# Gated cross-attention and top-2 expert layer on one Trainium2 core: a changed order of first maxima and weights, and a second expert product in rounded part and rest

## What is computed

```python
# attention with gate
Q, K, V = ln(x) @ Wq + bq, ctx @ Wk + bk, ctx @ Wv + bv      # 16 heads of 16
attn = softmax(Q @ K.T / sqrt(16))
x = x + tanh(g_xattn) * ((attn @ V) @ Wo + bo)
# experts with gate
xf = ln(x)
scores = softmax(xf @ w_router.T); weights, idx = top_k(scores, 2)
h = silu(xf @ w1[e]) * (xf @ w3[e]); y = h @ w2[e]           # e over the two experts
x = x + tanh(g_ffn) * sum(weights * y)
```

## Time and profile before

| | us |
|---|---|
| median of 3 runs | 851.28 (850.83 to 853.52) |
| the profiled execution | 846.11 |
| its span | 844.4 |
| attention, from the first exponents to the last values | about 43 to 560 |
| expert tiles | about 560 to 836 |
| PE busy | 805.9 (95%) |
| DVE, ACT, POOL busy | 489.9, 441.4, 525.0 |

### The profile page before, as it was taken

The page is one execution under the profiler, slowest core; times in us unless marked ns, Lnnn a source line. Parts: engine busy times, 40 slices in busy tenths (PEclk is TensorE's granted clock), DMA queues, the critical chain, the costliest instruction groups (busy, mean ns, idle before and its releaser), DMA issues.

```text
span 844.4 us, 22220 instructions
## 1 busy us (share of the span) xinstructions
PE 805.9 (95%) x7529; PEld 698.5 (83%) x7529; DVE 489.9 (58%) x1170; ACT 441.4 (52%) x1120; POOL 525.0 (62%) x599
## 2 busy tenths in 40 slices
PE   7889999999999999999999999889999999999994
PEld 6789998999999999999999998767777777777773
DVE  5566777877777777777777777634622222222221
ACT  3356676676676677677666766555222222222221
POOL 6555565476667657666665765346677765656652
PEclk8989999999999999999999999999999999999998
DMA  5867777786676666676557566764443444434432
GB/s 158 191 150 174 197 185 192 180 205 156 171 176 158 169 165 158 153 178 154 136 147 175 139 156 138 213 146 79 57 60 62 75 64 64 64 62 65 64 57 30
DMA packets 99845, 112.33 MB, mean 133 GB/s; under 512 B 29276, under 2 KB 81124, under 8 KB 99736
## 3 DMA queue, kind: packets, MB, share of 16 engines
q1 hardware_dynamic: 79720, 92.48, 44.2%
q0 software_dynamic: 18512, 17.60, 13.5%
q10 hardware_dynamic: 1504, 0.85, 0.4%
HBM read 35.48 MB, written 17.53 MB: 63 GB/s over the span
## 4 chain that ended last, share of the span: by engine, by line
PE 78%; DVE 14%; issue 3%; DMA 2%; SPq 1%; ACT 1%; POOL 1%; ACTq 0%; POOLq 0%; DVEq 0%
PE ps L1474 18%; PE ps L1535 10%; PE ps L1198 9%; PE ps L1215 9%; PE ps L1229 7%; DVE negmax L922 7%; PE ps L1183 7%; PE ps L1330 3%; PE ps L1389 3%; PE ps L1222 3%; PE ps L1493 2%; PE ps L1418 2%; PE ps L1322 1%; DVE xa L907 1%; PE ps L1304 1%
## 5 line engine op out<-in xcount | busy, mean ns | idle before, releaser
L922 DVE TENSOR_REDUCE negmax<-ps 112x2 f32<-112x750 f32 x256 | 239.8, 938 | 110.4 <-PE ps L1215 109.2
L623 ACT ACTIVATE probs<-ps 125x448 f32<-125x448 f32 x384 | 209.6, 547 | 67.6 <-PE ps L1183 63.1
L402 POOL DMA_DIRECT2D stack<-negmax_t x128 | 68.0, 535 | 164.3 <-ACT negmax_t L678 153.1
L1183 PE MATMUL ps<-stack 97*125 97x224 f32 x768 | 166.5, 299 | 2.6 <-DMA stack<-negmax_t 1.8
L1215 PE MATMUL ps<-stack 96*112 96x376 f32 x512 | 140.5, 356 | 12.6 <-DVE negmax L922 11.8
L526 POOL DMA_INDIRECT out_dram<-y,idx x63 | 100.8, 1600 | 70.0 <-issue 30.9
L1183 PEld LDWEIGHTS ps<-stack 97*125 97x125 f32 x768 | 125.3, 189 | 9.3 <-DMA stack<-negmax_t 1.9
L722 ACT ACTIVATE silu<-ps 128x352 f32<-128x352 f32 x63 | 29.3, 465 | 184.4 <-PE ps L1474 184.4
L1134 DVE TENSOR_TENSOR h<-silu,ps 128x352 f32<-128x352 f32 x63 | 32.8, 521 | 147.3 <-PE ps L1474 147.2
L1535 PE MATMUL ps<-w_sb,h_t 128*128 x378 | 92.3, 380 | 0.7 <-ACT h_t L728 0.7
L1215 PEld LDWEIGHTS ps<-stack 96*112 96x112 f32 x512 | 71.5, 177 | 22.9 <-DVE negmax L922 19.8
(11 more groups left out here) (239 smaller groups left out, 1514.3 us busy)
## 6 DMA issues: line engine op xcount, KB each, us to landing
stack<-split SPq DMA_DIRECT2D x252, 150.0 KB, 2.9
stack<-split SPq DMA_DIRECT2D x127, 94.0 KB, 2.6
ctx_raw<-in_ctx_dram SPq DMA_DIRECT2D x29, 375.0 KB, 3.8
stack<-split SPq DMA_DIRECT2D x127, 56.0 KB, 2.8
out_dram<-xa SPq DMA_DIRECT2D x32, 112.0 KB, 2.5
xn_scratch<-xn SPq DMA_DIRECT2D x32, 112.0 KB, 2.2
xa<-in_x_dram SPq DMA_DIRECT2D x7, 448.0 KB, 4.2
w_sb<-in_L_ffn_w_dram SPq DMA_DIRECT2D x16, 176.0 KB, 2.8
```

The costliest lines, as they stand in the source:

```text
L402: gp.dma_start(dst[:, :, SKP + SQ * h:SKP + SQ * h + SQ], negmax_t[4 * h:4 * h + 4, half, :].bitcast(f32)).then_inc(s_nmrow[half][c % NSLO ...
L623: act.activation(probs[:, n % NP, :], ps[0:KW, EXPB + k % 2, 0:4 * SQ], ACT.Exp).then_inc(s_exp, 1)
L922: dve.tensor_reduce(negmax[:, half, :, p4], ps[0:SQ, m1:m2 + 1, 0:SK], axis=AX.X, op=ALU.max, negate=True).then_inc(s_max, 1)
L1183: last = pe.matmul(ps[0:KW, EXPB + k % 2, QW * m:QW * m + QW], stack[:, place_of(b), p, KW * ch:KW * ch + KW], stack[:, place_of(b), p, SK ...
```

## The change

Three parts. (1) In sub-step 0 of each step `maxes(c, 0)` goes ahead of `exps(b, 0)`. (2) The weights: w3's second half waits until the first half of the last batch's maxima rows has landed (three experts of it, the rest also for the end of batch 30's exponents); w2's first chunk is no longer loaded there, but with the other two chunks in step 31; PE waits for w1 alone ahead of its first w1 product, and for w3 ahead of the first w3 product. (3) From tile 13 on (50 of the 63) the second product is made from float32r parts: w2 is split once, in tiles 4 to 11, an expert at a time, by ACT (`w2_h`, a rounded copy, two instructions) and DVE (`w2_l`, the rest, two instructions); for each tile ACT's copy of the turned h is rounded (`ht_h`), DVE writes the rest (`ht_l`), and PE makes nine matmuls: ht_h with w2_h, ht_h with w2_l, ht_l with w2_h. To make room, `ctx_l`, `ctx_h`, `ctx_raw` and `probs` join the tensors whose memory is reused.

```diff
+        ctx_l, ctx_h = (late.enter_context(nc.sbuf_tensor(n, [P, NSLOT, DC, SKP], f32r)) for n in ("ctx_l", "ctx_h"))
+        ctx_raw = late.enter_context(nc.sbuf_tensor("ctx_raw", [P, DC, SK], f32))
+        probs = late.enter_context(nc.sbuf_tensor("probs", [KW, NP, 4 * SQ], f32))
         late.close()
...
+        ht_h, ht_l = (sb(n, [P, FC, P], f32r) for n in ("ht_h", "ht_l"))
+        w2_h, w2_l = (sb(n, [P, FC, NE, EMB], f32r) for n in ("w2_h", "w2_l"))
...
+        SPLIT, PARTS = 4, 13
...
+        def w2_parts(e):
+            n = F - P * (FC - 1)
+            return [tuple(w[:, 0:FC - 1, e, :] for w in (w2_sb, w2_h, w2_l)), tuple(w[0:n, FC - 1, e, :] for w in (w2_sb, w2_h, w2_l))]
...
@@ SP @@
                     sp.wait_ge(s_stack[(B - 1) % NSLOT], stacked(B - 1))
+                    sp.wait_ge(s_w13, 16 * DC * NE)
                     for e in range(NE):
                         sp.dma_start(w3_lo[:, e, :], w3[e, 0:P, :]).then_inc(s_w13, 16)
-                    first_weights()
+                    sp.wait_ge(s_exp_ps, 12 * (B - 2) + 6)
+                    sp.wait_ge(s_nmrow[0][(B - 1) % NSLOT], 32 * ((B - 1) // NSLOT + 1))
+                    for e in range(NE):
+                        if e == 3:
+                            sp.wait_ge(s_exp_ps, 12 * (B - 1))
+                        sp.dma_start(w3_hi[:, e, :], w3[e, P:2 * P, :]).then_inc(s_w13, 16)
...
                     sp.wait_ge(s_nmrow[1][(B - 1) % NSLOT], 32 * ((B - 1) // NSLOT + 1))
-                    for c in range(1, FC):
+                    for c in range(FC):
@@ ACT @@
-                    act.activation(h_t[:, :, :], ps[:, HTB, 0:FC * P], ACT.Copy).then_inc(s_h_t, 1)
+                    if t - 1 < PARTS:
+                        act.activation(h_t[:, :, :], ps[:, HTB, 0:FC * P], ACT.Copy).then_inc(s_h_t, 1)
+                    else:
+                        act.activation(ht_h[:, :, :], ps[:, HTB, 0:FC * P].rearrange("p (c q) -> p c q", c=FC), ACT.Copy).then_inc(s_h_t, 1)
+                if 0 <= t - SPLIT < NE:
...
+                    for raw, high, low in w2_parts(t - SPLIT):
+                        act.activation(high, raw, ACT.Copy).then_inc(s_w2h, 1)
@@ DVE @@
+                if t - 1 >= PARTS:
+                    dve.wait_ge(s_h_t, t)
+                    dve.tensor_tensor(ht_l[:, :, :], ps[:, HTB, 0:FC * P].rearrange("p (c q) -> p c q", c=FC), ht_h[:, :, :].bitcast(f32),
+                                      ALU.subtract).then_inc(s_htl, 1)
                 if t < TILES:
                     dve.wait_ge(s_silu, t + 1)
...
+                if 0 <= t - SPLIT - 1 < NE:
+                    for n, (raw, high, low) in enumerate(w2_parts(t - SPLIT - 1)):
+                        dve.wait_ge(s_w2h, 2 * (t - SPLIT - 1) + n + 1)
+                        dve.tensor_tensor(low, raw, high.bitcast(f32), ALU.subtract).then_inc(s_w2l, 1)
@@ PE @@
+                    if k == 0 and c is not None:
+                        maxes(c, 0)
                     if b is not None:
                         exps(b, k)
-                    if k in MAX_IN and k != 5 and c is not None:
+                    if k in MAX_IN and k not in (0, 5) and c is not None:
                         maxes(c, MAX_IN.index(k))
...
-                        pe.wait_ge(s_w13, 16 * 4 * NE)
+                        pe.wait_ge(s_w13, 16 * DC * NE)
...
+                    wait(pe, s_htl, o - PARTS)
                     for c in range(FC):
                         last = pe.transpose(ps[:, HTB, P * c:P * c + P], h[:, P * c:P * c + P], ident[:, :])
...
+                    if m == 0:
+                        pe.wait_ge(s_w13, 16 * 2 * DC * NE)
                     inner(m, (w3_lo, w3_hi), BB, e_m, s_b)
...
-                        pe.wait_ge(s_w2, 16 * (NE + FC - 1))
+                        pe.wait_ge(s_w2, 16 * FC)
                         pe.wait_ge(s_pv_t, B)
                     pe.wait_ge(s_h_t, o + 1)
                     wait(pe, s_y, o)
-                    for c in range(FC):
-                        n = min(P, F - P * c)
-                        last = pe.matmul(ps[:, YB, 0:EMB], h_t[0:n, c, :], w2_sb[0:n, c, bass.ds(e_o, 1), :].rearrange("p e d -> p (e d)"),
-                                         start=(c == 0), stop=(c == FC - 1))
+                    if o == PARTS:
+                        pe.wait_ge(s_w2l, 2 * NE)
+                    wait(pe, s_htl, o - PARTS + 1)
+                    terms = ((h_t, w2_sb),) if o < PARTS else ((ht_h, w2_h), (ht_h, w2_l), (ht_l, w2_h))
+                    for j, (ht, w) in enumerate(terms):
+                        for c in range(FC):
+                            n = min(P, F - P * c)
+                            last = pe.matmul(ps[:, YB, 0:EMB], ht[0:n, c, :], w[0:n, c, bass.ds(e_o, 1), :].rearrange("p e d -> p (e d)"),
+                                             start=(j + c == 0), stop=(j == len(terms) - 1 and c == FC - 1))
                     last.then_inc(s_y_ps, 1)
```

More of the change, by code:

```diff
@@ L69, in flamingo @@
         half2, lnv2, lnr2, lnt2 = (sb(n, [SQ, 1]) for n in ("half2", "lnv2", "lnr2", "lnt2"))
-        ctx_l, ctx_h = sb("ctx_l", [P, NSLOT, DC, SKP], f32r), sb("ctx_h", [P, NSLOT, DC, SKP], f32r)
         xn, xn_t = sb("xn", [SQ, EMB]), sb("xn_t", [P, DC, SQ])
@@ L78, in flamingo @@
         NP = 14
-        probs = sb("probs", [KW, NP, 4 * SQ])
         pv_t = sb("pv_t", [P, 4, SQ])
@@ L113, in flamingo @@
         iota_i = staged[0][:, 2560:2560 + P].bitcast(i32)
-        ctx_raw = sb("ctx_raw", [P, DC, SK])
         pad_tab = w1_sb[0:ROWS // 256, 0].rearrange("p e f -> p (e f)")[:, 0:4 * P].bitcast(i32).rearrange("p (a b c) -> p a b c", a=2, c=2)
@@ L134, in flamingo @@
         s_x = [sem(f"s_xload{n}") for n in range(4)]
+        s_w2h, s_w2l, s_htl = sem("s_w2h"), sem("s_w2l"), sem("s_htl")
         s_chi, s_clo, s_whi, s_wlo = (sem(n) for n in ("s_chi", "s_clo", "s_whi", "s_wlo"))
@@ L266, in load_idx @@
                              ).then_inc(s_idx_in[t % NIS], 16)
-            def first_weights():
-                for n in range(2 * NE):
-                    sp.wait_ge(s_exp_ps, 12 * (B - 2) + 3 * n // 4 + 1)
-                    e = n % NE
-                    if n < NE:
-                        sp.dma_start(w3_hi[:, e, :], w3[e, P:2 * P, :]).then_inc(s_w13, 16)
-                    else:
-                        sp.dma_start(w2_sb[:, 0, e, :], w2[e, 0:P, :]).then_inc(s_w2, 16)
             for i in range(FIRST, LAST + 1):
@@ L727, in _ @@
                     wait(act, s_y_ps, t - 1)
-                    act.activation(h_t[:, :, :], ps[:, HTB, 0:FC * P], ACT.Copy).then_inc(s_h_t, 1)
+                    if t - 1 < PARTS:
[3 more added lines that the diff above has]
+                if 0 <= t - SPLIT < NE:
+                    if t == SPLIT:
+                        act.wait_ge(s_pv, 4 * B)
+                        act.wait_ge(s_w2, 16 * FC)
+                    for raw, high, low in w2_parts(t - SPLIT):
+                        act.activation(high, raw, ACT.Copy).then_inc(s_w2h, 1)
                 if t == 3:
```

## The result

The changed kernel takes 872.05 us (median of 4 runs, 871.38 to 872.57) against 851.06 (4 runs) for the kernel before, run beside it: ratio 1.0246 (95% interval 1.0218 to 1.0274), 21.0 us slower. Its profiled execution took 872.02 (span 870.3).

A forecast was written before the change was run, and what follows sets the result against it. PE was taken to bound the steady tiles (busy 197.00 of 197.00 us). Terms -0.3 + 1.9 + 0.6 + 12 + 0.5 = +14.7 us, added to the median 851.28, gave 866.0, range 849 to 877.

The forecast's parts named there:

- the main term: Late tiles' w2 product from float32r parts: sequencer sends behind the wait for DVE's rest lengthen each tile, +12 us.
- The w2 product from parts, +12: Tiles 13 to 62: nine sends, read and address follow the wait; +0.25 in 48 turns, outer bounds -1 to +35.
- The first rival: Late tiles: sequencer is not the bound, PE's shorter work sets the period; total 844 to 849, chance 0.20.
- The weights, +1.9: Transition from attention to tiles: w2 lands near 573.1 against use at 571.22; +1.9 us, bounds -1.5 to +6.
- late next: First w2 product: w2's later landing cancels the about 1 us kept from the earlier maxima's rows.
- The price of the third chunk, 3.2: Transition: 1024 KB more of w2 in the same stretch delay its landing by 3.2 us, plus 0.6 for SP's later start.
- its 1.80 and 2.45: PE's transition waits before the change: 1.80 for the last maxima's rows, 2.45 inside the values with no releaser.
- the second rival: Transition: w2 later still, PE stands some 5 us, clock falls to 1.2 GHz; total 872, chance 0.12.
- First maxima, -0.3: Attention steps: DVE's queue hides the earlier product except in batch 31; -0.3 us, bounds 0 to -1.
- Splitting w2, +0.6: Tiles 4 to 12: DVE's extra subtractions partly reach the path in tiles 7 to 9; +0.6 us, bounds 0 to 1.2.
- Tail, +0.5: Last two w2 products: each waits for DVE's rest with nothing beside it, but is 0.24 shorter; +0.5 us.
- The base: Sum made against the profiled execution of 846.11, 5.2 below the median 851.28; that difference was taken over.

The follow-up runs named there:

- more reads: Kernel before, with two further unused reads of the expert's number ahead of each tile's own from tile 14 on; 896.69 us, ratio 1.0547.
- read ahead: Changed kernel, with the read of the next tile's expert number moved ahead of the waits before the nine w2 products; 850.72 us, ratio 1.0014.
- with the maxima: Changed kernel without the w2 split and the product from parts, keeping maxima order and weights order; 846.84 us, ratio 0.9949 to the kernel before.
- weights alone: Kernel before, with only the new order of the weight loads, w3 awaited at its first product; 847.82 us, ratio 0.9959.
- w3 behind the rows: Changed kernel, both waits moved, index loads first, three w3 second-half experts ahead of the first maxima's rows, five behind the second half's; 836.76 us, ratio 0.9827.
- maxima first: Kernel before, with only the first maxima's product moved ahead of the first exponents; 851.77 us, ratio 1.0010.

## Why the prediction was right or wrong

The sign and the mechanism of the main term were right: 866.0 forecast, 872.05 measured, slower, by the sequencer behind the new wait. Two terms were off, with opposite signs: the tiles by some +12, the weights by some -6. The total is nearer than its parts deserve; with the weights at their forecast it would be about 877, at the upper end of the range. That much of it is luck.

- **The w2 product from parts, +12: measured +23.6.** The mechanism is the one given, a series of rest, sends, read and load. Three of its numbers held: DVE's rest 0.59 after ht_h's end, the read 0.75, the load 0.1 behind w1's address. Two failed. From the rest's end to the first address 0.04 was taken, as in the kernel before, and 0.01 for one more semaphore; but the wait for the rest stands in a semaphore instruction of its own ahead of the address (776.14 and 776.25), and the first address comes 0.15 after ht_l. And the nine sends took 0.73 from the first address to the read, not 0.64: I had taken two array instructions as worth 0.02 less than four, but in this trace an address instruction has a pitch of 0.12 though fewer follow it, the register kind one of 0.11 to 0.13. These are about 0.1 and 0.09 a tile on top of 0.25. The rest of the way to 0.49 (225.9 less 202.2 over 48) is a few longer tiles. +0.49 lies outside the +0.1 to +0.4 given, inside its outer bounds; the mean period of 4.71 is just beyond the 4.7 from which the prediction calls its prices of the sends wrong, the median of 4.66 below it. Its 0.37 for the three old sends holds for most tiles; in the tile of the earlier trace rows they took 0.41. The signs in the profile came out as named, a gap of 0.34 ahead of w1's load put down to issue and the period of most tiles up to 12 unchanged; the number's read comes 1.47 after ht_h's end, where some 1.2 was named.
- **The first rival (the sequencer is not the bound)** is refuted by the kernel with more reads. The sentence that the rows show no work queued across the wait was a misreading of the earlier trace rows. The trace with the read ahead has at least eleven loads queued. The Trainium skill (TensorE: Matmul & The Clock Gate, the table at its head) gives the engine a queue 64 deep; the trace agrees as far as it goes, and the depth of 64 no run here shows. The queue did not help all the same. What the array could still do during the wait was the work sent before it, here the rest of w3's product; the number's read and w1's address stand behind the wait. I took a deep queue for the rival's case; the queue is there, and the rival is wrong.
- **The weights, +1.9: -3.5 alone by the ratio, -4.3 with the maxima.** The step that failed is that w2, "late next", is paid in full and gives the term its sign. In the changed kernel's trace PE never waits for w2; in that of the weights alone it does, for 1.60, near the lateness forecast. The price of the third chunk, 3.2, was somewhat high: from the first of its issues to its last landing w2 took 14.4 us in the kernel before, 15.9 in the one trace of the new order that has the landings (w3 behind the rows, with five experts of w3 ahead of it) and 16.7 in that of the weights alone, if PE's wait ended with the landing; that is +1.5 and +2.3. I weighed the term against a trace in which the old order had met no fall of the clock, and took its 1.80 and 2.45 as the old order's usual cost. The other traces of the old order have 39.1 and 41.7 for the stretch. What stands in place of the +1.9 is a gain that comes with a higher mean granted clock (0.986 against 0.981); which part of the transition holds it, the traces don't settle.
- **The clock** fell to 1.2 GHz for part of the transition in the changed kernel, as the second rival had it, but not behind w2: it was low from about 552 on, and ahead of that PE had waited 1.01 for DVE and 1.53 for the rows. That part of the rival, a stand of 5 us for w2, did not come. The time that it gave, 872, is right by chance: the 6 us over the forecast are the tiles', less what the weights gain.
- **First maxima, -0.3: right**, 1.0010 (0.9989 to 1.0031). DVE turns the step, the array only moves its wait: PE's median wait at the second maxima goes from 0.29 to 0.07, and one of 0.22 comes at the first.
- **Splitting w2, +0.6: +0.3** from the first w2 product to that of tile 12. **Tail, +0.5: +0.1.**
- **The base.** The sum was made against an execution 5.2 below the median. Between the two traces the change costs 25.9, between the medians 21.0. The traced execution of the kernel before met no fall of the clock in the transition (37.1 us for the stretch, 39.1 in the kernel with more reads, the same up to there); that this makes the difference is likely, and not shown.

## What to carry to other kernels

While TensorE's sequencer stands at a wait, nothing behind it in the program gets done: addresses, reads of registers, sends all follow in series. So put a wait directly ahead of the first instruction that needs it, and reads that need no data ahead of it: one moved line turned +2.5% into -1.6% here. Where the array is at its limit, look up how long the sequencer takes from its last wait to the next product's load, and count an instruction that works out an address (0.12 us here) as dear as a small matmul. A stretch with many waits on DMA is judged by many runs, not by one trace.

## What the runs showed of the hardware

- An address instruction of PE's sequencer has a pitch of 0.12 us, an operation on a register 0.11 to 0.13, a read of a number from memory 0.65 until a second read behind it and 0.75 until the first address behind it (late tiles of the changed kernel and of that with more reads); a float32r product of 256 columns 0.12. By these numbers a product with an address of its own would just keep up, an estimate: none of the kernels has nine of them.
- A wait ahead of an address stood in the sequencer, for the rest in a semaphore instruction of its own 0.11 ahead of the address; the wait for the rest ahead of a product with no address was carried by the weight load, and cost the sequencer nothing that shows (sends of 0.73 in both kernels).
- The sequencer runs at least eleven loads with their matmuls ahead of the array (read ahead: the read at 749.5, w3's last load at 751.5).
- The second half of the last maxima's rows (DMAs of 1.8 KB) landed 1.8 to 3.1 us after its last issue without weights on the DMA engines beside it, 3.8 to 5.1 with them.
- In three traces of twelve (w3 behind the rows, more reads, maxima first) TensorE's signals for the first turned rows came 3.2 to 3.8 us after the recorded end of the product, and ACT and DVE stood for them, for 2.6 to 5.3 us, in the stretch in which w2 is loaded; the cause is open.
- The mean granted clock of single executions of one kernel ran from 0.973 to 0.985 (kernel before, 16 executions), and a microsecond of clock lost went with 0.4 to 0.8 us of time.
